# Weight splits moved ahead in the queues, W products and levels of the last chunks reordered

## The reference

```python
# attention layer, H = 16 heads, keys of 64, values of 16, LV = 12 levels
Q, K, V, dl = x @ Wq.T, x @ Wk.T, x @ Wv.T, x @ Wdl.T
dt  = softplus(x @ Wdt.T + dt_bias);  cg = cumsum(-exp(A_log) * dt)
Lam = softplus(Lp * dl)
Wmat[t, s] = Q[t].K[s] / 8 * exp(cg[t] - cg[s]) * Lam[t, level(t, s)]   # s <= t
o = (Wmat @ V) @ Wout.T + x
x = layernorm(x + layernorm(o) * ln_g + ln_b)
# recurrent layer
for t in (0, 1):
    f, i = sigmoid(x[t] @ wf.T + c @ uf.T + bf), sigmoid(x[t] @ wi.T + c @ ui.T + bi)
    g    = tanh(x[t] @ wc.T + c @ uc.T + bc)
    c    = f * c + i * g
h = tanh(x @ wo.T + c @ uo.T + bo)
out = layernorm(x + h)
```

## Time and profile before

| what | value |
|---|---|
| median of three runs | 690.88 us |
| the profiled execution | 691.23 us |
| its span in the trace | 689.4 us |
| PE busy | 667.5 us (97%) |
| DVE, ACT, POOL busy | 473.2, 339.6, 348.2 us |

### The profile page before, as it was taken

The page is one execution under the profiler, slowest core; times in us unless marked ns, Lnnn a source line. Parts: engine busy times, 40 slices in busy tenths (PEclk is TensorE's granted clock), DMA queues, the critical chain, the costliest instruction groups (busy, mean ns, idle before and its releaser), DMA issues.

```text
span 689.4 us, 22147 instructions
## 1 busy us (share of the span) xinstructions
PE 667.5 (97%) x9194; PEld 604.7 (88%) x9194; DVE 473.2 (69%) x1072; ACT 339.6 (49%) x759; POOL 348.2 (51%) x471
## 2 busy tenths in 40 slices
PE   9799999999999999999999999999978999999994
PEld 7699999999999999899999999999967888888894
DVE  3854877769786868667696868688896435454546
ACT  5545454445545554444455455545433434555555
POOL 2705555646465565656364655655455125343434
PEclk9999999999999999999999999999987899999998
DMA  8112130303131221203031212213032000000002
GB/s 303 40 45 58 41 88 11 98 7 94 30 70 41 60 57 42 68 2 98 8 91 32 68 48 52 69 31 82 3 98 63 1 1 1 31 31 31 31 32 92
DMA packets 53588, 37.09 MB, mean 54 GB/s; under 512 B 5360, under 2 KB 52080, under 8 KB 53488
## 3 DMA queue, kind: packets, MB, share of 16 engines
q1 hardware_dynamic: 53488, 35.67, 19.0%
HBM read 30.41 MB, written 5.24 MB: 52 GB/s over the span
## 4 chain that ended last, share of the span: by engine, by line
PE 90%; DVE 3%; ACT 2%; SPq 1%; DMA 1%; POOL 1%; issue 1%; POOLq 0%; DVEq 0%; ACTq 0%
PE bank L383 66%; PE bank L386 6%; PE bank L407 5%; PE bank L474 5%; PE bank L439 5%; PE bank L503 4%; SPq L330 1%; DMA xt<-in_wffn 1%; DVE t L982 1%; ACT t L751 0%; DVE st L1279 0%; DVE hh L979 0%; DMA scr<-cT 0%; DVE t L979 0%; ACT QT L751 0%
## 5 line engine op out<-in xcount | busy, mean ns | idle before, releaser
L383 PE MATMUL bank<-xH,wH 128*128 128x256 f32 x480 | 144.6, 301 | 0.0
L383 PE MATMUL bank<-xL,wH 128*128 128x256 f32 x480 | 135.0, 281 | 0.0
L383 PE MATMUL bank<-xH,wL 128*128 128x256 f32 x480 | 134.3, 280 | 0.0
L979 DVE TENSOR_TENSOR W<-bank,E 128x512 f32<-128x512 f32 x128 | 82.2, 684 | 34.7 <-PE bank L383 34.7
L383 PEld LDWEIGHTS bank<-xH,wH 128*128 128x128 f32 x480 | 90.5, 189 | 6.3 <-issue 5.5
L383 PEld LDWEIGHTS bank<-xL,wH 128*128 128x128 f32 x480 | 90.7, 189 | 0.4
L383 PEld LDWEIGHTS bank<-xH,wL 128*128 128x128 f32 x480 | 90.5, 188 | 0.0
L751 ACT ACTIVATE E<-bank 128x512 f32<-128x512 f32 x128 | 66.1, 603 | 49.0 <-PE bank L407 49.0
L751 ACT ACTIVATE QT<-bank 128x512 f32<-128x512 f32 x64 | 38.2, 596 | 100.7 <-PE bank L383 100.7
L383 PE MATMUL bank<-QT,KT 64*128 64x128 f32 x1024 | 65.9, 278 | 1.2 <-ACT E L751 1.2
L383 PEld LDWEIGHTS bank<-QT,KT 64*128 64x128 f32 x1024 | 59.7, 188 | 5.6 <-ACT E L751 1.5
(11 more groups left out here) (151 smaller groups left out, 1686.9 us busy)
## 6 DMA issues: line engine op xcount, KB each, us to landing
cB<-scr SPq DMA_DIRECT2D x240, 64.0 KB, 2.9
xt<-in_xT SPq DMA_DIRECT2D x16, 256.0 KB, 3.0
xs<-in_x SPq DMA_DIRECT2D x16, 256.0 KB, 3.2
out<-xs SPq DMA_DIRECT2D x16, 256.0 KB, 2.1
xt<-in_wffn SPq DMA_DIRECT2D x8, 256.0 KB, 3.1
QT<-in_wqk SPq DMA_DIRECT2D x4, 256.0 KB, 5.8
KT<-in_wqk SPq DMA_DIRECT2D x4, 256.0 KB, 6.1
scr<-cT SPq DMA_DIRECT2D x16, 64.0 KB, 1.9
```

Source lines behind the costliest of these rows:

```text
L383: return e.matmul(o, a, b, start=start, stop=stop)
L979: return e.tensor_tensor(o, a, b, op)
```

## The change

The eight splits move to steps 112 to 119 (FIRST_SPLIT = NG - 16), in the order SPLIT of the columns with which the last projections are done; each waits for its projection. Loads 2 to 6 stand in SP's queue ahead of the coefficients of superchunk 15, load 7 between the coefficients of chunk 30 and those of chunk 31. For chunks 30 and 31 DVE makes both halves of W at s % 4 == 1. POOL's levels of chunk 31 go from step 121 to 119, and `turn_levels` of chunk 31 runs on DVE at step 121, behind W and ahead of the inter part.

```diff
--- before.py
+++ after.py
@@ -42,11 +42,17 @@
 STEPS = range(-3, NG + 13)
 FIRST_FFN = NG - 1
 
+FIRST_SPLIT = NG - 16
+SPLIT = [0, 4, 1, 5, 2, 6, 3, 7]
+
 
 def token_jobs(s):
 
     out = []
     for d, j in ((12, 7), (0, 0), (0, 1), (1, 2), (3, 8), (5, 3), (7, 4), (8, 5)):
+        if j == 7 and s > NG - 12:
+
+            d = 10
         n = s + 11 - d
         if n % 8 == 0 and (0 if j == 7 else 1) <= n // 8 < NSG:
             out.append((n // 8, j))
@@ -309,9 +315,11 @@
             def load_xt(sg):
                 e.dma_start(xt[sg % 2][:, :, :], kt(xT)[:, :, 256 * sg:256 * sg + 256]).then_inc(l_xt[sg % 2], 16)
 
-            def load_wf(n):
-                e.dma_start(xt[n % 2][:, :, :], wffn.rearrange("(k p) w n -> p k w n", p=P)[:, :, n, :]).then_inc(
-                    l_xt[n % 2], 16)
+            def load_wf(i):
+                if i >= 2:
+                    e.wait_ge(g_wf, i - 1)
+                e.dma_start(xt[i % 2][:, :, :], wffn.rearrange("(k p) w n -> p k w n", p=P)[:, :, SPLIT[i], :]).then_inc(
+                    l_xt[i % 2], 16)
 
             def load_coefs(sg):
 
@@ -321,6 +329,8 @@
                 e.wait_ge(l_sc, 16 * sg + 16)
                 for c in range(2):
                     ci = 2 * sg + c
+                    if ci == NC - 1:
+                        load_wf(7)
                     if ci in INTER:
                         if ci >= 2 and ci - 2 in INTER:
                             for h in range(2):
@@ -350,6 +360,9 @@
             e.wait_ge(p_proj, 8)
             load_xt(2)
             for sg in range(NSG):
+                if sg == NSG - 1:
+                    for i in range(2, 7):
+                        load_wf(i)
                 load_coefs(sg)
                 if sg + 3 < NSG:
                     e.wait_ge(g_xl, sg + 1)
@@ -359,9 +372,6 @@
                 if sg >= NSG - 3 and sg < NSG - 1:
                     e.wait_ge(g_xl, sg + 1)
                     load_wf(sg - NSG + 3)
-            for n in range(2, 8):
-                e.wait_ge(g_wf, n - 1)
-                load_wf(n)
             for n in range(16):
                 e.wait_ge(a_out, n + 1)
                 if n == 15:
@@ -591,7 +601,7 @@
             def first_bias():
 
                 e.wait_ge(a_qk, 8 * NSG)
-                e.wait_ge(g_wf, UC + 1)
+                e.wait_ge(g_wf, 7)
                 e.wait_ge(g_c0, 1)
                 for mt in range(2):
                     for n in range(3):
@@ -845,11 +855,10 @@
                         e.wait_ge(p_st, STATE[ci - 1] + 1)
                     act(Kt[:, 512 * n:512 * n + 512], MB[m][:, :], ACT.Copy).then_inc(m_free[m], 1)
 
-            def split_ffn(n):
-                e.wait_ge(l_xt[n % 2], wf_landed(n))
-                if n == 0:
-                    e.wait_ge(p_proj, 8 * NSG)
-                act(wH[:, :, wcol(n)], xt[n % 2][:, :, :], ACT.Copy).then_inc(a_wf, 1)
+            def split_ffn(i):
+                e.wait_ge(l_xt[i % 2], wf_landed(i))
+                e.wait_ge(p_proj, 8 * (NSG - 1) + i + 1)
+                act(wH[:, :, wcol(SPLIT[i])], xt[i % 2][:, :, :], ACT.Copy).then_inc(a_wf, 1)
 
             def turn_block(blk, t):
                 i = blk % 2
@@ -952,8 +961,8 @@
                         turn_coefs(sg)
                 for sg, j in token_jobs(s):
                     tokens(sg, j)
-                if 0 <= s - NG + 9 < 8:
-                    split_ffn(s - NG + 9)
+                if 0 <= s - FIRST_SPLIT < 8:
+                    split_ffn(s - FIRST_SPLIT)
                 for u in units_at(s):
                     if u[0] == "x" and u[2] == 0:
                         gate(*u[1:])
@@ -1304,11 +1313,17 @@
             for s in STEPS:
                 if (ci := chunk_at(s, 5)) is not None:
                     turn_y(ci)
-                if 0 <= s < NG and s % 4 in (1, 2):
+                if 0 <= s < NG - 8 and s % 4 in (1, 2):
                     weights(s // 4, s % 4 - 1)
+                if NG - 8 <= s < NG and s % 4 == 1:
+
+                    weights(s // 4, 0)
+                    weights(s // 4, 1)
                 for sg, j in token_jobs(s - 1):
-                    if j in (5, 7):
+                    if j == 5 or j == 7 and sg < NSG - 1:
                         turn_levels(2 * sg + (j - 5) // 2)
+                if s == NG - 7:
+                    turn_levels(NC - 1)
                 if (ci := chunk_at(s, 6)) is not None:
                     out_proj(ci)
                 if s == FIRST_FFN:
@@ -1490,10 +1505,11 @@
                 if (ci := chunk_at(s, 9)) is not None:
                     e.wait_ge(d_mv2, ci + 1)
                     root(rs2[:, :], lr2[:, :], mv2[:, 1:2], g_rs2)
-                if 0 <= s - NG + 9 < 8:
-                    n = s - NG + 9
-                    e.wait_ge(a_wf, n + 1)
-                    tt(wL[:, :, wcol(n)], xt[n % 2][:, :, :], wH[:, :, wcol(n)], ALU.subtract).then_inc(g_wf, 1)
+                if 0 <= s - FIRST_SPLIT < 8:
+                    i = s - FIRST_SPLIT
+                    c = wcol(SPLIT[i])
+                    e.wait_ge(a_wf, i + 1)
+                    tt(wL[:, :, c], xt[i % 2][:, :, :], wH[:, :, c], ALU.subtract).then_inc(g_wf, 1)
 
 
 def constants():
```

## The result

The changed kernel takes 692.69 us in the median of ten runs (691.90 to 694.86), the kernel before 690.96 us beside it (690.21 to 691.87): 1.0027 times, with a 95% interval of 1.0016 to 1.0039. Run again beside other experiments it gave 1.0020 (1.0007 to 1.0033). By these ratios the change is slower by 1.4 to 1.9 us. The forecast was 691.6 us, with a range of 688.6 to 693.6 and 0.7 us slower than before: the time lies in the range, and the slowdown is larger than forecast. The prediction called up to 0.2% the same and gave that 0.50, against 0.30 for slower; 1.0027 and 1.0020 lie just beyond that bound and on it.

A forecast was written before the change was run, and what follows sets the result against it. PE was taken as busy nearly everywhere, with stops of 3.80 and 1.23 us at the change-over from attention to recurrent stage. Removing them was paid back by new waits: +0.7 us net, 691.6 us forecast, range 688.6 to 693.6.

The forecast's parts named there:

- region: From exponents of chunk 28 to scores of chunk 31; forecast 0.7 us longer, everything behind it taken as equal.
- (a): Splits at steps 112 to 119: first seven loads keep up, costed at nothing; exponents of chunk 30 0.5 us late, covered.
- (b): SP's queue: load 7 issued behind chunk 30's eight coefficient issues, landing 3.5 us later, at 509.5 us.
- (c): ACT's queue: E of chunk 30 waits behind split 7; PE stands 4.6 us, scores of chunk 30 start at 511.15.
- (d): Clock after PE's stop: scores of chunk 30 take 3.7 us at half clock, ending at 514.85.
- (e): DVE's new order: 5.65 us from scores 30's end to weigh; new 0.9 us wait for oo, scores 31 at 522.55.
- rival 3: Load 7 lands late, 4.7 us after issue: everything behind is 1.2 us later, 692.8 us; chance 0.18.
- (f): Sum at scores of chunk 31: 522.55 - 521.85 = +0.7 us, everything from there on costed at nothing.
- rival 2: Half clock behind the bias moves: shortened by a third, -1.7 us, 689.2 us; can be longer; chance 0.10.
- 1 (scores at full clock): Clock up by 511 us: scores of chunk 31 start at 520.9, -0.95 us, 689.9 us; chance 0.14.
- 4 (DVE held by GpSimd): Three DVE operations ahead of CT of chunk 29 held by POOL: +0.5 to +1.7, 692.1 to 693.3 us; chance 0.08.
- 5 (it does what it says, 684.2 us): Load 7 not in E's way: stops of 3.80 and 1.23 and about 2 us of half clock go; chance 0.05.

The follow-up runs named there:

- inter_first: split7_late with C and CT of chunk 31 behind the inter part of chunk 30 on DVE, still in step 121; 0.9959 of before (689.03 us).
- fill_clock: The changed kernel with nine added matmuls of 256 columns on PE between keys and scores of chunk 30, output unchanged; 1.0021 of before (691.29 us).
- split7_late: The changed kernel with the eighth split at the end of step 120, behind E of chunk 30, its load unmoved; 0.9982 of before (689.43 us).
- levels_121: inter_first with GpSimd's levels of chunk 31 back at step 121 and the eighth split at the end of step 121; 0.9921 of before (685.68 us).
- third_buffer: The changed kernel with a third buffer for the eighth matrix, its load ahead of all coefficients of superchunk 15; 0.9976 of before (690.15 us).
- wide_bias: levels_121 with the 36 bias products 80 columns wide instead of 2, result unchanged; 0.9938 of before (687.23 us).

## Why the prediction was right, and where it was off

The direction held, and the mechanism nearly step by step; the size was too small. The forecast of the region was 0.7 us longer than before, and it came out 1.4 and 1.8 us longer. Times after the start of the exponents of chunk 28:

| step | forecast | changed | changed, again |
|---|---|---|---|
| exponents 30 (a) | 28.95 | 29.07 | 29.06 |
| load 7 issued (b) | 31.60 | 31.18 | 32.31 |
| load 7 landed, split 7 starts (b) | 35.13 | 35.55 | 36.00 |
| scores 30 start (c) | 36.78 | 37.21 | 37.65 |
| scores 30 end, T (d) | 40.48 | 40.93 | 41.36 |
| weigh 30 (e) | 46.13 | 46.68 | 47.12 |
| scores 31 (e) | 48.18 | 48.84 | 49.27 |

The end of scores 30 is read as the start of PE's next product.

(a) was right: PE doesn't stop anywhere between 475 and 499 us, and CT of chunk 30 comes 0.6 us late (a stop of 0.92 for 0.30), which is covered by the longer stop behind it. The reason is the one given, GpSimd's queue: its subtraction (497.50) stands ahead of Vw, AT and prod, and DVE waits 0.44 us for prod.

(b) is the term that was mis-sized. From issue to the start of the split it took 4.37 and 3.69 us; I took 3.5 from the one load that I had for its like. In the ten profiles in which load 7 stands between the coefficients of chunks 30 and 31 it took 3.4 (inter_first) to 4.7 us (fill_clock), and 3.5 in split7_late, so one load could not tell the size, and where 3.5 was met it was luck. Part of the spread is the issue itself: 1.14 us in the first profile and 0.43 in the second, and counted from its end the split starts 3.2 to 3.3 us later in both. The issue also began 0.4 us earlier than forecast in the first profile and 0.7 us later in the second, where the eight coefficient issues ahead of it took 4.77 us and not 3.64. At the start of the split the changed kernel was 0.4 and 0.9 us behind the forecast, of the 0.7 and 1.1 us at scores 31. This was rival 3, and the truth lay between it and the forecast.

(c) was right: E behind the split, 1.66 us from the split's start to PE's scores, in both profiles (1.66 and 1.65). (d) was right, with 3.79 us of scores for the 3.7 scaled from the exponents.

(e) was right in its sum, T to weigh 5.75 us for 5.65, because DVE's chain, which decides it, came out as added up. The stop it forecast was not: PE's own path behind T took 5.55 us and not the 4.8 I gave, mostly because inter ran partly at half clock (2.31 for 1.59 us), although the forecast's own half clock, to about 516, reached into it. So the stop before weigh was 0.20 us and not 0.9. And the step had a hole: state of chunk 30 waits for DVE to have read the inter part out of its bank, which the new order puts behind CT, and no term stands for that. In the profiled run PE came just late enough for that wait to be invisible; in the second it is 0.35 us. That it cost so little here was luck: without the half clock ahead of it the stop was 1.07 us (fill_clock), and without the stop before the scores 2.75 (split7_late).

(f) For the rest, "costed at nothing" was right in the first pair of profiles (167.55 and 167.51 us). In the second profile it is 166.04, since the half clock behind the bias lasted from 533.3 to 540.2 instead of 530.0 to 540.3. This is rival 2, at 1.5 us for the 1.7 named there; it comes and goes between profiles of one kernel, and most variants here show the shorter one. The region was 0.43 us longer in that profile (49.27), so region and rest together are 1.0 us shorter than in the first.

The rivals: 1 (scores at full clock) didn't happen by itself, and where it was forced it brought 1.0 to 1.4 us in the trace, which the times don't show. 4 (DVE held by GpSimd) was right as a mechanism and wrong in its place: not at CT of chunk 29, where there was room, but between 504 and 511 us, where DVE has to be ready for W of chunk 30; under the stop of 4.9 us it was hidden. The rule of the Trainium skill ("GPSIMD Engine Reference", section 1, Specifications: interfaces shared with VectorE, contention for two SBUF inputs or a two-port mode) agrees with the traces of split7_late and levels_121: xs 1.25 and 0.41 us, oo 1.48 and 0.48. Which of the two conditions xs meets, with one tensor as input, no trace shows. 5 (it does what it says, 684.2 us) would have been wrong in its size even without the queued load: split7_late and third_buffer gave 689.4 and 690.2 us, and only with the order on DVE and GpSimd mended too did a version come near it (levels_121, 685.7 us).

levels_121 beats both kernels, at 0.9921 (0.9908 to 0.9933) of before. What its gain is made of: 3.8 us of region, and 1.7 us of a shorter half clock behind the bias products, which its profile shows and which I can't ascribe to its edits, as the kernel before has executions 1.7 us shorter too.

## What to carry to other kernels

A load issued between others is only as early as what stands ahead of it in the queue, and an engine that works in program order and waits for it holds everything behind it in its program: for each moved step ask what stands behind it on its engine, and when its input lands. When one stop of the bottleneck engine is removed, look for the next buffer release and the next in-order neighbour; here each of three mended waits (the load, the bank of the inter part, GpSimd beside DVE) uncovered the next, and they were worth 1.7 to 2.5, 0.4 and 2.7 us of the region in that order, of which the 0.4 is within the spread of two profiles. For differences of 0.2% compare stretches of the traces that start and end at the same instructions, because two profiles of one kernel differ by as much as the change does, and take more than one profile of each kernel: the same stretch differed by 0.43 us.

## What the runs showed of the hardware that I had not expected

A load of 256 KB landed 3.4 to 4.7 us after its issue with eight loads of 64 KB ahead of it and eight behind (ten profiles), against 3.1 us in the median of the eight of the kernel before (2.8 to 4.7). DVE's tensor_scalar of 128x256 went from 0.41 to 1.25 us beside a GpSimd tensor_tensor, and its scalar_tensor_tensor from 0.48 to 1.48, a price of 0.8 to 1.0 us for one operation; four products with one input in PSUM took 2.48 us beside the same two GpSimd operations and without them. A PE stop of 1.46 us was followed by half clock in one profile (wide_bias) and not in another with the same code up to there (levels_121). The half clock behind the bias products lasted 10.2 us in two of the three profiles of the two kernels compared and 6.8 us in the third.
